# Two-layer cross-attention kernel: softmax row sums sent through DRAM by DMA, and V's high and low parts side by side in one stationary tile

## What is computed

```
h = layernorm(x);  x = attention(h, h, a1_*) + x         # self attention, 256 keys
h = layernorm(x);  x = attention(h, context, a2_*) + x   # cross attention, 120 keys
h = layernorm(x);  x = feed_forward(h) + x               # u * gelu(gate), 256 -> 2*1024 -> 256
attention: 16 heads of 64, softmax(q k^T / 8) v, heads joined, times Wo, plus bo
```

## Time and profile before

| | |
|---|---|
| median of the runs | 1081.24 us |
| the profiled execution's own time | 1081.92 us |
| its span, first to last instruction | 1080.1 us |
| TensorE (PE) busy, share of the span | 988.0 us, 91% |
| DVE (VectorE), ACT (ScalarE), POOL (GpSimd) | 66%, 58%, 33% |
| chain that ended last: PE, DVE, ACT | 77%, 10%, 7% |

### The profile page before, as it was taken

How to read it: one execution, slowest core, us unless ns; L and a number is a source line. 1 busy time by engine, 2 the same in 40 slices (tenths; PEclk the granted TensorE clock), 3 DMA queues, 4 the chain that set the end, 5 groups by cost and what they waited for, 6 DMA issues and landing times.

```text
span 1080.1 us, 21165 instructions
## 1 busy us (share of the span) xinstructions
PE 988.0 (91%) x7776; PEld 927.1 (86%) x7776; DVE 712.8 (66%) x1610; ACT 625.8 (58%) x1945; POOL 356.5 (33%) x474
## 2 busy tenths in 40 slices
PE   4688775499999999999999999999999998899998
PEld 4577654389999999999989889999999998899998
DVE  3466745496767666767667885776677667666664
ACT  2566443286657565657566765766676667534343
POOL 1101323133333333333342343554454454401010
PEclk9999888699999999999999998999999999999999
DMA  6221000100300000000000300300000001000100
GB/s 206 68 68 34 26 20 20 44 11 2 97 3 21 1 21 1 22 1 21 2 21 2 103 18 9 104 25 2 25 26 10 17 21 58 12 30 21 41 30 20
DMA packets 30444, 34.60 MB, mean 32 GB/s; under 512 B 4360, under 2 KB 23816, under 8 KB 30344
## 3 DMA queue, kind: packets, MB, share of 16 engines
q1 hardware_dynamic: 30344, 33.26, 10.2%
HBM read 24.86 MB, written 8.39 MB: 31 GB/s over the span
## 4 chain that ended last, share of the span: by engine, by line
PE 77%; DVE 10%; ACT 7%; issue 2%; POOL 1%; DMA 1%; SPq 1%; DVEq 0%; POOLq 0%
PE bank L1324 14%; PE bank L1325 14%; PE bank L1326 14%; PE bank L1549 8%; PE bank L1532 5%; PE bank L1336 5%; PE bank L1590 3%; PE bank L1591 3%; PE bank L1592 3%; PE bank L1564 3%; ACT p L737 2%; PE bank L1440 1%; PE bank L1506 1%; DVE bn L903 1%; DVE hT_lo L1089 1%
## 5 line engine op out<-in xcount | busy, mean ns | idle before, releaser
L737 ACT ACTIVATE p<-bank,negmax 128x256 f32<-128x256 f32 (+1 forms) x512 | 208.2, 428 | 18.4 <-DVE negmax L1106 15.5
L554 POOL TENSOR_TENSOR oT_hi<-oT,ones 128x256 fp32r<-128x256 f32 x128 | 93.7, 732 | 370.7 <-DVE oT L1129 370.7
L747 ACT CAST pT_hi<-bank 128x512 fp32r<-128x512 f32 (+1 forms) x256 | 110.8, 486 | 166.1 <-PE bank L1549 165.9
L1324 PE MATMUL bank<-hT_hi,w_hi 128*128 128x256 f32 x640 | 190.8, 298 | 6.3 <-DVE hT_lo L1089 2.5
L1326 PE MATMUL bank<-hT_hi,w_lo 128*128 128x256 f32 x640 | 181.6, 284 | 0.0
L1325 PE MATMUL bank<-hT_lo,w_hi 128*128 128x256 f32 x640 | 181.4, 283 | 0.0
L1324 PEld LDWEIGHTS bank<-hT_hi,w_hi 128*128 128x128 f32 x640 | 122.7, 192 | 9.9 <-DVE hT_lo L1089 4.8
L1121 DVE TENSOR_TENSOR pT_lo<-bank,pT_hi 128x512 fp32r<-128x512 f32 (+1 forms) x256 | 129.9, 550 | 0.5
L1102 DVE TENSOR_REDUCE negmax<-bank 128x2 f32<-128x512 f32 x128 | 82.2, 684 | 66.8 <-PE bank L1532 66.8
L1325 PEld LDWEIGHTS bank<-hT_lo,w_hi 128*128 128x128 f32 x640 | 123.1, 192 | 0.0
L1326 PEld LDWEIGHTS bank<-hT_hi,w_lo 128*128 128x128 f32 x640 | 122.8, 192 | 0.0
(11 more groups left out here) (202 smaller groups left out, 2737.8 us busy)
## 6 DMA issues: line engine op xcount, KB each, us to landing
w_stage<-in_weights SPq DMA_DIRECT2D x47, 256.0 KB, 4.5
x_in<-x_dram SPq DMA_DIRECT2D x24, 256.0 KB, 2.9
x_dram<-x_out SPq DMA_DIRECT2D x16, 256.0 KB, 3.2
l_x<-in_x SPq DMA_DIRECT2D x4, 512.0 KB, 5.0
x_dram<-l_out SPq DMA_DIRECT2D x4, 512.0 KB, 2.8
out_dram<-x_out SPq DMA_DIRECT2D x8, 256.0 KB, 3.1
w_stage<-in_weights SPq DMA_DIRECT2D x9, 128.0 KB, 5.1
l_ctx<-in_ctx SPq DMA_DIRECT2D x4, 180.0 KB, 4.4
```

The source lines that it names most:

```text
L554: nc.gpsimd.tensor_tensor(oh[:, G % PAIRS, :], of[:, :], ones[:, :], ALU.mult).then_inc(y["o_hi"], 1)
L737: last = nc.scalar.activation(p[:, G % 2, e, t * cols:(t + 1) * cols], scores_at(G, e, t), ACT.Exp, bias=negmax[:, G % 2, t, e:e + 1], acc ...
L747: nc.scalar.copy(pTh[0:r, G % 2, e, 0:n], bank[4 + e][0:r, 0:n]).then_inc(y["pT_hi"], 1)
L1324: nc.tensor.matmul(dst, lh, rh, start=(i == 0), stop=False)
```

## The change

Two things are changed together.

**V side by side.** V's high and low parts lie in one buffer `v_hi_lo`. A head has one stationary tile of 128 columns: head 0 is (high, low), head 1 is (low, high). One pass with pT_hi and one with pT_lo per key tile gives high*p in one half of the partitions and low*p in the other. Each head has its own half of bank 6. ACT then copies the two low halves to SBUF, changing partitions (`copy_low_values`), and DVE adds them to the high halves (`add_low_values`); this sum is not yet normalised. `weighted_values` has 8 matmuls per self step (12 before) and 4 per cross step (6 before), and adds low*low as a fourth product. The zeros between the heads go.

**Row sums through DRAM.** POOL's widening, PE's two transposes and ACT's copy of them go. SP writes the reciprocals of a pair (128 partitions x 2 heads x 2 values) to DRAM in step G (`send_sums`, pieces of 8 bytes), and in step G+1, behind the next write, reads them back, broadcast over 64 partitions for each head (`spread_sums`, two DMAs). POOL multiplies (a new first instruction in `split_o`), and then splits as before. SP's loads, stores and weight loads are spread over the steps between these DMAs.

```diff
-VW = 3 * DH
+VW = 2 * DH
...
-        def v_dst(buf, b, c):
-            half = slice(c % 2 * 4 * VW, (c % 2 + 1) * 4 * VW)
-            return buf[0:v_rows(b), c // 2, half].rearrange("p (g s d) -> p g s d", g=4, s=3)[:, :, 0:3:2, :]
+        def v_dst(b, c, low):
+            part = vv[0:v_rows(b), c // 2, c % 2 * 4 * 2 * VW:(c % 2 + 1) * 4 * 2 * VW]
+            part = part.rearrange("p (g s d) -> p g s d", g=4, s=4)
+            return part[:, :, 1:3, :] if low else part[:, :, 0:4:3, :]
...
+            def send_sums(G):
+                sp.wait_ge(y["rsum"], G + 1)
+                if G >= 2:
+                    sp.wait_ge(y["rT"], 32 * (G - 1))
+                sp.dma_start(sums_dram[G % 2, :, :].rearrange("e (q t) -> q e t", t=NT),
+                             rs[:, G % 2, :].rearrange("q (e t) -> q e t", e=2)).then_inc(y[f"rsum_row{G % 2}"], 16)
+            def spread_sums(G):
+                sp.wait_ge(y[f"rsum_row{G % 2}"], 16 * (G // 2 + 1))
+                if G >= 2:
+                    sp.wait_ge(y["o_norm"], G - 1)
+                for e in range(2):
+                    sp.dma_start(rT[e * DH:(e + 1) * DH, G % 2, :], sums_dram[G % 2, e:e + 1, :].partition_broadcast(DH)
+                                 ).then_inc(y["rT"], 16)
             load(0)
             load_context(B)
             load(1)
-            load(2)
-            for b in range(3 * B):
-                if b + 3 < 3 * B:
-                    load(b + 3)
-                store(b)
...
+            for G in range(STEPS):
+                b, i = divmod(G, PAIRS)
+                send_sums(G)
+                if G >= 1:
+                    spread_sums(G - 1)
+                if i == 3 and b >= 1:
+                    store(b - 1)
+                if i == 4:
+                    load(b + 2)
+                if i == 5 and B < b + 2 < 2 * B:
+                    load_context(b + 2)
+                if b == 1 and i < 4:
+                    load_weights(sp, 12 + i, 13 + i)
...
+                if b == 2 * B - 1 and i in (6, 7):
+                    load_weights(sp, 18 + i, 19 + i)
+            sp.wait_ge(y["rT"], 32 * (STEPS - 1))
+            spread_sums(STEPS - 1)
+            store(2 * B - 1)
+            for b in range(2 * B, 3 * B):
+                if b + 2 < 3 * B:
+                    load(b + 2)
                 store(b)
...
-            def widen_sums(G):
...
             def split_o(G):
+                pool.wait_ge(y["o_sum"], G + 1)
+                pool.wait_ge(y["rT"], 32 * (G + 1))
+                if G >= 1:
+                    pool.wait_ge(y["o_lo"], G)
+                nc.gpsimd.tensor_tensor(on[:, :].rearrange("p (t q) -> p t q", t=NT),
+                                        of[:, G % 2, :].rearrange("p (t q) -> p t q", t=NT),
+                                        rT[:, G % 2, :].rearrange("p (q t) -> p t q", t=NT),
+                                        ALU.mult).then_inc(y["o_norm"], 1)
...
-            def copy_rT(G):
-                act.wait_ge(y["o"], G + 1)
-                nc.scalar.copy(rT[:, :], bank[6][:, S:2 * S]).then_inc(y["rT_copied"], 1)
+            def copy_low_values(G):
+                act.wait_ge(y["o"], G + 1)
+                if G >= 1:
+                    act.wait_ge(y["o_sum"], G)
+                nc.scalar.copy(ob[0:DH, :], bank[6][DH:128, 0:S])
+                nc.scalar.copy(ob[DH:128, :], bank[6][0:DH, S:2 * S]).then_inc(y["o_low"], 1)
...
             def inverse_sums(G):
                 dve.wait_ge(y["exp"], 2 * G + 2)
+                if G >= 2:
+                    dve.wait_ge(y[f"rsum_row{G % 2}"], 16 * (G // 2))
...
-            def normalise_o(G):
-                dve.wait_ge(y["rT_copied"], G + 1)
-                if G >= 1:
-                    dve.wait_ge(y["o_lo"], G)
-                nc.vector.tensor_tensor(of[:, :], bank[6][:, 0:S], rT[:, :], ALU.mult).then_inc(y["o_norm"], 1)
+            def add_low_values(G):
+                dve.wait_ge(y["o_low"], G + 1)
+                if G >= 2:
+                    dve.wait_ge(y["o_norm"], G - 1)
+                nc.vector.tensor_tensor(of[0:DH, G % 2, :], bank[6][0:DH, 0:S], ob[0:DH, :], ALU.add)
+                nc.vector.tensor_tensor(of[DH:128, G % 2, :], bank[6][DH:128, S:2 * S], ob[DH:128, :], ALU.add
+                                        ).then_inc(y["o_sum"], 1)
...
-            for v_ in (vh, vl):
-                for pr in range(PAIRS):
-                    last = nc.vector.memset(v_[:, :, pr * VW + DH:pr * VW + 2 * DH].bitcast(F32), 0.0)
-            last.then_inc(zeros_ready, 1)
...
             def weighted_values(G):
...
-                pe.wait_ge(y["rsum_wide"], G + 1)
...
                 if G >= 1:
-                    pe.wait_ge(y["o_norm"], G)
-                for t in range(NT):
-                    nc.tensor.transpose(bank[6][:, S + t * 128:S + (t + 1) * 128], rsw[:, G % 2, t, :], ident[:, :])
...
+                    pe.wait_ge(y["o_sum"], G)
                 pe.wait_ge(y["pT_lo"], 2 * G + 2)
                 pe.wait_ge(y["v_lo"], values_until(b, g))
-                product(bank[6][:, 0:S], terms).then_inc(y["o"], 1)
+                for e in range(2):
+                    dst = bank[6][:, e * S:(e + 1) * S]
+                    for j in range(tiles):
+                        vs = vv[0:r, j, (2 * g + e) * VW:(2 * g + e + 1) * VW]
+                        pc = slice(j * S, (j + 1) * S)
+                        nc.tensor.matmul(dst, vs, pTh[0:r, G % 2, e, pc], start=(j == 0), stop=False)
+                        last = nc.tensor.matmul(dst, vs, pTl[0:r, G % 2, e, pc], start=False, stop=(j == tiles - 1))
+                last.then_inc(y["o"], 1)
```

More of the change, by code:

```diff
@@ L223, in build @@
                 qkl = sb("qkT_lo", [128, PAIRS, 2, S], F32R, where=att)
-                vh = sb("v_hi", [128, NT, PAIRS * VW], F32R, where=att)
-                vl = sb("v_lo", [128, NT, PAIRS * VW], F32R, where=att)
+                vv = sb("v_hi_lo", [128, NT, HEADS * VW], F32R, where=att)
                 p = sb("p", [128, 2, 2, NT * S], where=att)
@@ L231, in build @@
                 rs = sb("rsum", [128, 2, NT * 2], where=att)
-                rsw = sb("rsum_wide", [128, 2, NT, 2 * DH], where=att)
-                rT = sb("rsumT", [128, S], where=att)
-                of = sb("oT", [128, S], where=att)
+                rT = sb("rsumT", [128, 2, S], where=att)
+                ob = sb("oT_low_values", [128, S], where=att)
+                of = sb("oT", [128, 2, S], where=att)
+                on = sb("oT_scaled", [128, S], where=att)
                 oh = sb("oT_hi", [128, PAIRS, S], F32R, where=att)
@@ L270, in build @@
             "cT_hi", "cT_lo", "qk", "qk_hi", "qk_lo", "v", "v_hi", "v_lo", "scores", "negmax", "exp", "rsum",
-            "rsum_wide", "pT", "pT_hi", "pT_lo", "o", "rT_copied", "o_norm", "o_hi", "o_lo", "wo", "up", "gelu", "glu",
+            "rsum_row0", "rsum_row1", "rT", "pT", "pT_hi", "pT_lo", "o", "o_low", "o_sum", "o_norm", "o_hi", "o_lo", "wo", "up", "gelu", "glu",
             "f_hi", "f_lo", "down")}
         NI = B // L0B
+        sums_dram = nc.dram_tensor("rsums_dram", (2, 2, S), F32, kind="Internal").ap()
         def wcols(name, kt, lo_col, n):
@@ L803, in step_self @@
                 if G >= 1:
-                    copy_rT(G - 1)
+                    copy_low_values(G - 1)
             def step_cross(G):
@@ L1113, in inverse_sums @@
                 dve.wait_ge(y["exp"], 2 * G + 2)
-                nc.vector.reciprocal(rs[:, G % 2, :], expsum[:, G % 2, :, :].rearrange("p t e -> p (t e)")
+                if G >= 2:
+                    dve.wait_ge(y[f"rsum_row{G % 2}"], 16 * (G // 2))
+                nc.vector.reciprocal(rs[:, G % 2, :].rearrange("p (e t) -> p e t", e=2), expsum[:, G % 2, :, :].rearrange("p t e -> p e t")
                                      ).then_inc(y["rsum"], 1)
@@ L1210, in step_self @@
                 if G >= 1:
-                    normalise_o(G - 1)
+                    add_low_values(G - 1)
             def step_cross(G):
```

46 lines of the change are left out of this document (13 added, 33 removed).

## The result

The changed kernel took **1087.66 us** (1086.24 to 1090.02, five runs) against 1081.17 for the kernel before on the same chip: ratio 1.0064, 95% interval 1.005 to 1.0079, slower by 0.6%. Forecast were 1044.5 us, range 1026 to 1063, and a chance of 0.04 for slower.

A forecast was written before the change was run, and what follows sets the result against it. PE was taken to bound self attention and, with holes, cross attention. The profiled 1081.9 us minus 44.8 (self), minus 8 (cross), plus 16 (clock falls) gives 1045.1; the runs' median is 0.7 lower: 1044.5 us, range 1026 to 1063.

The forecast's parts named there:

- PE's part of self attention: Self attention, PE: fewer matmuls and no transposes ahead save 0.70 us a step, 44.8 us over 64 steps.
- I take the upper, nearest in form: DVE's additions and ACT's copies over 64 partitions cost like 128-partition pairs: +0.33 us and +0.27 us a step.
- So I cost it at nothing: Self attention, worst step i = 3: DVE's 5.8 us in a 5.6 us PE step is made up later, costing nothing.
- The wait at i = 4: Cross attention, PE's wait for DVE's sum grows from 1.10 us to about 2.5 us in a middle batch.
- the wait at i = 1: Cross attention, PE at the output projection waits 1.0 us for POOL's `oT_lo`; the gain of steps 0 and 1 goes.
- I take three or four of the six: Batches 9 to 14: longer i = 4 waits drop the clock to 1.2 GHz, 4.6 us each, 16 us in all.
- rival C: Cross attention: clock falls in all six middle batches and one or two more, 1056 to 1063 us; chance 0.11.
- Nothing waits: POOL and the DMAs: sums return 4.2 us after DVE's reciprocal, POOL needs them five to seven later, so no wait.
- the 4.2 us: Sums' round trip from DVE's reciprocal: 0.5 for the write's issue, 1.0 for two reads, 2.7 to land.
- the three marks that I gave for being wrong: POOL waits for `rT`, self stage above 372 us, or clock full in all six middle cross batches.
- a rival with two falls a batch: Cross attention: waits at i = 1 and i = 4 both drop the clock, 64 us against 53 saved, 1092; chance 0.04.
- rival E: Sums come late at pair 7: 8-byte pieces take 3 us more than any row, 1075 us; chance 0.05.

The follow-up runs named there:

- DMA alone: Changed kernel with V in the old layout, no ACT copy, one DVE multiplication by ones over 128 partitions, sums still through DRAM: 1083.78 us.
- The pairs over 128 partitions: Changed kernel with ACT's two copies and DVE's two additions each over 128 partitions, halves not mixed, V's summed low part left out: 1071.94 us.
- the spare matmuls: Changed kernel plus unused matmuls on PE ahead of its wait for the sum at i = 4 (in batch 15, i = 4 to 7): 1074.61 us, ratio 0.995.
- an edit worth 3 to 4 us alone: Changed kernel with four DRAM rows for the sums and a counter for each parity, so SP needn't wait for the last reads: 1083.97 us.
- the kernel without the low part: Changed kernel with no ACT copies and one DVE multiplication of 128 rows by ones, V's low part and second head's values left out: 1066.64 us.
- the hybrid without spare matmuls: Changed kernel with V side by side in self attention only, the layout of before in cross attention, sums by DMA in both: 1066.1 us, ratio 0.9867.
- the filled kernel without the low part: Changed kernel with no ACT copies, one DVE multiplication of 128 rows by ones, plus unused PE matmuls ahead of the i = 4 wait: 1053.09 us.

## Why the prediction was wrong

**PE's part of self attention: right.** Eight weighted-value matmuls take 0.96 us and nothing stands ahead of them; a middle batch gave 5.3 us of the 5.6 forecast. DMA alone gave 1.7 of it, the layout the rest.

**"I take the upper, nearest in form" (+0.33 us for the additions, +0.27 for the copies): the first step that failed.** I called the price of a pair of 128-partition instructions the upper bound. It is not. DVE's additions cost +0.69 up to the row maxima, and ACT's copies 0.38 + 0.38 us where the one copy of before held the next instruction off by 0.26 (L751, 761.13 to 761.39), +0.50. Instructions over halves of the partitions don't overlap with their neighbours. The pairs over 128 partitions show it. What they don't separate is whether it's the number of partitions or the one they start at, nor, for ACT, the change of partitions. The Trainium skill, "VectorE: DVE Perf Modes", Two Vector instructions with no wait between them, gives the start as the reason, as a model: an instruction is held until all earlier ones have finished if an input begins in another group of 32 partitions than in the last instruction that read the same memory, or its output in another than in the last that wrote it. By that rule the second addition (partition 64), the reciprocal and the row maxima (back to 0) are held; the trace has 0.43, 0.46 and 0.21 us before the next start, against 0.34, 0.33 and 0.09 where all start at 0. It agrees. For ACT the 0.38 against 0.27 us is what the runs show. And the trace of before had a row that is nearer in form than the one I chose, on DVE:

```profile
767.83 1.31 DVE L1152 TENSOR_TENSOR qkT_lo<-bank,qkT_hi 64x480 fp32r<-64x480 f32 x2
```

Two instructions of 64 partitions and 480 columns took 1.31 us, twice the 0.66 of another operation over 128 partitions and that many columns. Read beside the pair of 128 partitions in the earlier trace rows, 0.75 us for two of 0.42, it says that halves don't overlap.

**"So I cost it at nothing" (cover on DVE and ACT): the second.** I compared sums of busy time with the length of the stage, and took DVE's term alone for the path. But copies and additions are in series: both lie in a ring of row maxima, exponentials, rounding, copies and additions, 4.55 us long in the changed kernel. The steps i = 4 and 1 of a cross batch went from 2.9 and 3.7 us to 4.1 and 4.6. Of the two pairs DVE's is the one whose cost is shown by itself, 0.66 to 0.69 us at i = 0, 1 and 3; ACT's copies taken out alone gave a batch nothing. In batches 0 and 7 (13.7 us of the miss) the pairs are worth 6.0 us: without both, these batches took 43.0 and 51.1 us against 46.0 and 54.1. 1.5 us more is the short fall of the clock in batch 0. For the other 6.2 us no run shows a cause; the forecast took 5.6 us off batch 7 as off the others, although it was 2.6 us longer than they in the kernel before and PE waited 1.5 us in it for DVE's `qkT_lo`. The ring also took the gain of i = 5 to 7 in the cross batches: forecast -1.3 us for these three steps, measured 5.2 + 4.5 + 4.1 with the spare matmuls against 5.5 + 4.4 + 4.1 before, -0.2. A batch at a full clock took 38.2 us, not 35.5: 2.7 us, six times, 16 us of the miss. Without the pairs it took 35.3.

**The wait at i = 4: right in place and nearly in size** (2.15 to 2.25 in five of six batches, 2.5 forecast), the wait at i = 1 too (1.2 in two batches, 1.0 forecast).

**"I take three or four of the six": mis-sized.** The clock fell in all six, and in batches 8 and 15 and at the start of the feed-forward besides, as in rival C. A fall cost about 3 us a batch (38.2 with the spare matmuls against 41.4 without), not 4.6, which was read at batch 8, where DVE also splits weights. That the ring, which the clock doesn't lengthen, covers part of it is likely, and wasn't tried. Six of these make 19, so the term of 16 came out near by two errors against each other. Rival C's 1056 to 1063 was still 25 us too low, for the reasons above.

**"Nothing waits" (POOL and the DMAs): wrong, and hidden.** POOL waited 45 times for the sums, 120.7 us in all. The landings were as forecast (2.8 us for the reads, 3.3 for the write); what the 4.2 us left out was the wait that the change itself adds ahead of the write on SP. In the changed kernel it cost only 3 to 4 us, because PE waited elsewhere anyway. With the other two causes gone the same wait cost 16, partly by the waits of DVE for the write, which the forecast doesn't have either. Two of the three marks that I gave for being wrong were there: POOL waiting for `rT`, and a self stage above 372 us (380.3, against 409.5 before).

In sum, by parts of the table: batches 0 and 7 13.7 us, middle self batches 2.0, batch 8 3.2, batches 9 to 14 19.7, batch 15 and behind it 3.8, together 42.4 less 0.3 at the start, for the 42 between -36.8 forecast and +5.4 measured in the profiled executions. I had the slower side at 0.04, by a rival with two falls a batch. It was one fall a batch and a longer ring.

What stays open: the 6.2 us of batches 0 and 7; what ACT's copies cost when the clock is kept; why the clock falls behind some waits and not behind others of the same length; and what of the 2.4 us behind the last step is due to the late last landing and what to the short fall of the clock there. None was tried by itself.

## To carry to other kernels

Before a PE instruction is taken away, look for the ring of instructions on the other engines that repeats each step, and add up the *start-to-start* distances along it; shares of busy time don't show it. An operation split over two halves of the partitions cost its full duration twice here. And where PE gets ahead, ask what its longer wait does to the clock: here 16 matmuls a batch that nobody needs (24 in batch 8, 64 in batch 15), put ahead of the wait, were worth 13 us, and three causes each hid behind the others, so that an edit worth 3 to 4 us alone was worth 16 when the two others were gone.

## What the runs showed that I had not expected

- The length of a wait doesn't tell by itself whether the clock falls. In the changed kernel each wait at i = 4 of batches 9 to 14 (1.72 to 2.25 us) was followed by 7 to 10 us at 1.2 GHz, and in the kernel without the low part each of 1.52 to 2.10 us; the 1.10 us of the kernel before never were the earlier trace rows. In the hybrid without spare matmuls the clock fell behind 1.29 and 1.54 us and held behind 1.34, 1.34 and 1.40; in the DMA form alone it fell behind 1.43 us and held behind 1.72. It also held behind waits at the output projection (for `oT_lo`) of 2.73 us in that hybrid and of 1.92 us in the filled kernel without the low part.
- A kernel doesn't get faster by all that it leaves out: without the low part it took 1066.64 us, and the hybrid without spare matmuls, which computes everything, 1066.1.
- A write of 2 KB in pieces of 8 bytes landed 3.3 us after its issue, against 2.7 us for the 64 KB load of the earlier trace rows. No run has the same write in larger pieces, so what the small ones cost isn't shown; the 3 us more than any row that rival E counted with did not come.
